# Attention kernel on one Trainium2 core: in four turns of eighteen two key tiles are weighed together, first halves first

## What is computed

```
q, k, v = Wq @ gn(x), Wk @ gn(x), Wv @ gn(x)      # per head: 64 x 2304
attn = softmax(q^T k)                             # 2304 x 2304, no scale
out  = gamma * (attn @ v^T) + Wsc @ gn(x)
y    = x + out
```

## Time and profile before

| | us |
|---|---|
| median of 3 runs | 3061.2 (3058.46 to 3061.65) |
| the profiled execution, its time | 3061.98 |
| the profiled execution, its span | 3060.3 |
| TensorE (PE) busy | 2967.9 (97%) |
| GpSimd (POOL) busy | 2765.5 (90%) |
| VectorE (DVE) busy | 2249.1 (73%) |
| ScalarE (ACT) busy | 1939.8 (63%) |

### The profile page before, as it was taken

The page is one execution under the profiler, slowest core; times in us unless marked ns, Lnnn a source line. Parts: engine busy times, 40 slices in busy tenths (PEclk is TensorE's granted clock), DMA queues, the critical chain, the costliest instruction groups (busy, mean ns, idle before and its releaser), DMA issues. The chain is left out here.

```text
span 3060.3 us, 149786 instructions
## 1 busy us (share of the span) xinstructions
PE 2967.9 (97%) x69035; PEld 2242.4 (73%) x69035; DVE 2249.1 (73%) x2856; ACT 1939.8 (63%) x3156; POOL 2765.5 (90%) x2039
## 2 busy tenths in 40 slices
PE   7999999999999999999999999999999999999998
PEld 4677777777777777777777777777777777777765
DVE  7777677777787767777777767777777777777774
ACT  4565676766566667676656567667666666666555
POOL 1798899999899999999989889999999989999898
PEclk9999999999999999999999999999999999999999
DMA  3111111111112011111011101111010101110101
GB/s 133 32 42 41 31 47 25 47 35 26 35 47 56 24 38 42 34 48 30 21 41 52 48 24 44 38 34 48 21 30 21 30 21 30 22 30 21 30 21 31
DMA packets 169076, 112.71 MB, mean 37 GB/s; under 512 B 120320, under 2 KB 166400, under 8 KB 168448
## 3 DMA queue, kind: packets, MB, share of 16 engines
q1 hardware_dynamic: 168448, 103.13, 12.8%
HBM read 56.10 MB, written 18.87 MB: 24 GB/s over the span
## 5 line engine op out<-in xcount | busy, mean ns | idle before, releaser
L984 POOL TENSOR_TENSOR PLO<-PE 128x768 f16<-128x768 f32 x1727 | 2531.7, 1479 | 226.0 <-ACT PE L613 203.5
L786 DVE TENSOR_REDUCE mx<-MX 128x2 f32<-128x768 f32 x1728 | 1654.6, 958 | 727.0 <-PE MX L444 705.2
L613 ACT ACTIVATE PE<-SL 128x768 f32<-128x768 f32 x1728 | 1400.4, 810 | 1020.2 <-PE SL L470 1020.1
L505 PE MATMUL OB<-V,PE 64*128 64x129 f16 x20736 | 1403.8, 219 | 1.2
L502 PE MATMUL OB<-V,PLO 64*128 64x65 f16 x20736 | 1307.1, 190 | 0.0
L505 PEld LDWEIGHTS OB<-V,PE 64*128 64x128 bf16 x20736 | 1034.4, 94 | 238.4 <-PE OB L502 82.9
L470 PE MATMUL SL<-QK 64*128 64x384 f16 x10368 | 1142.8, 324 | 11.7 <-ACT PE L613 6.5
L502 PEld LDWEIGHTS OB<-V,PLO 64*128 64x128 f16 x20736 | 968.9, 95 | 141.6 <-issue 0.2
L391 PE MATMUL PJ<-X,WT 64*128 64x384 f16 x6624 | 941.0, 323 | 0.0
L444 PE MATMUL MX<-QK 64*128 64x384 f16 x3456 | 579.4, 326 | 46.7 <-DVE mx L786 36.5
L470 PEld LDWEIGHTS SL<-QK 64*128 64x128 f16 x10368 | 440.6, 94 | 180.9 <-ACT PE L613 19.3
(11 more groups left out here) (108 smaller groups left out, 913.8 us busy)
## 6 DMA issues: line engine op xcount, KB each, us to landing
gx<-x SPq DMA_DIRECT2D x36, 768.0 KB, 4.7
xr<-x SPq DMA_DIRECT2D x96, 192.0 KB, 2.4
out<-xr SPq DMA_DIRECT2D x96, 192.0 KB, 1.9
X<-x SPq DMA_DIRECT2D x6, 768.0 KB, 8.5
CR<-c SPq DMA_TRANSPOSE x96, 2.3
back<-half SPq DMA_TRANSPOSE x95, 2.9
QK<-wk SPq DMA_DIRECT2D x1, 1024.0 KB, 12.7
QK<-wv SPq DMA_DIRECT2D x1, 1024.0 KB, 13.4
```

The source lines that it names most:

```text
L505: last = pe.matmul(acc, upper, v, start=begin, stop=False, skip_group_check=True)
L613: act.activation(PE32[:, s % PB, :].rearrange("p (h n) -> p h n", h=2), SL[:, :, 0:CH], ACT.Exp, scale=1.0 / SS).then_inc(s_exp, 1)
L786: nc.vector.tensor_reduce(mx3[:, n % 2, :, k], MX[:, :, 0:CH], AX.X, ALU.max).then_inc(s_mxf, 1)
L984: nc.gpsimd.tensor_tensor(PLO[:, s % PB, :], PE32[:, s % PB, :], PE32[:, s % PB, :].bitcast(BF16)[:, 1:4 * CH:2], ALU.subtract).then_inc(s ...
```

## The change

In a turn k of `STARTS`, TensorE now does score, part 0 of tile s-3, `top`, part 0 of tile s-2, slots. In the turn behind it (1, 5, 10, 14) it does score, part 1 of tile s-4, `top`, slots, part 1 of tile s-3. Both first halves have the same sides, and so have both second halves. `side` and `started` keep the side: a crossing, with its wait, comes only where part 1 has the side of its own part 0. In turn 2, part 1 moves from before the first slot to behind it. `PB` goes from 4 to 5.

```diff
-PB = 4
+PB = 5
...
+            started, side = {}, [0]
...
-                else:
-                    pe.wait_ge(s_half, s + 1)
-                cross = (s + part) % 2
+                    started[s] = side[0]
+                elif side[0] == started[s]:
+                    pe.wait_ge(s_half, len(started))
+                    side[0] = 1 - side[0]
+                cross = side[0]
...
-                    if s >= LAG:
-                        weigh(s - LAG, 0)
-                    if U < TOPS:
-                        top(U)
-                    if s >= LAG and (lo == 0 or k == 2):
-                        weigh(s - LAG, 1)
+                    if lo == 0:
+                        if s >= LAG:
+                            weigh(s - LAG, 0)
+                        if U < TOPS:
+                            top(U)
+                        if s >= LAG:
+                            weigh(s - LAG + 1, 0)
+                    elif k - 1 in STARTS:
+                        if s > LAG:
+                            weigh(s - LAG - 1, 1)
+                        if U < TOPS:
+                            top(U)
+                    else:
+                        if s >= LAG:
+                            weigh(s - LAG, 0)
+                        if U < TOPS:
+                            top(U)
                     for i in range(lo, hi):
+                        if k == 2 and i == lo + 1 and s >= LAG:
+                            weigh(s - LAG, 1)
                         slot(4 * n + b, i)
-                    if s >= LAG and not (lo == 0 or k == 2):
+                    if s > LAG and k != 2 and lo:
                         weigh(s - LAG, 1)
```

## The result

| | before, us | after, us |
|---|---|---|
| median of 4 runs each | 3059.83 (3058.18 to 3061.65) | 3038.91 (3038.01 to 3040.84) |
| span of the profiled execution | 3060.3 | 3039.1 |

The ratio is 0.9932, with a 95% interval of 0.992 to 0.9945: 21 us or 0.7% faster. The forecast was 3046 us, 15 us faster, with a range of 3032 to 3056. The changed kernel ran again with the experiments, ten times: medians 3042.36 (ratio 0.9942, 0.993 to 0.9955) and 3044.05 (0.9947, 0.9933 to 0.9961). Over all 14 runs its median is 3041.5 us, so the gain is 18 to 21 us.

The account below looks back on a forecast made before the run. TensorE's order of work sets the pace, with two turns of every chunk held by another engine. 69 typical chunks x 0.22 = 15 us off 3061.98 gives 3047, median 0.8 lower: 3046 us, range 3032 to 3056.

Parts of the forecast that it names:

- The crossing: TensorE's weight loads wait for OB's own matmuls between part 0 and part 1; covering this saves 0.07 us a turn.
- Turn 9 given back in turn 12: GpSimd's chain holds turn 12's top, so turn 9's 0.07 us comes back as waiting; worth 0.00 to 0.01.
- Turn 2 held in turn 3: OB's evacuation chain ends 0.16 us later against TensorE, turn 3's part 0 waits 0.05; worth about 0.01.
- A typical chunk: Gains 0.07 x 3 (turns 13, 0, 4) + 0.01 (turn 2) + 0.00 (turn 9) = 0.22 us.
- Behind a conversion chunk: In 18 chunks turn 0 waits 0.47 us for GpSimd, absorbed by turn 8's top wait: 0, bounds -0.34 and +0.12.
- The last six chunks: Few slots; score waits for the exponential in 41 places and that loop sets their turns: gain 0.
- Five buffers: Exponential of s waits for part 1 of tile s-5, ended two turns earlier at latest: free; with four not.
- A: Every exposed crossing comes back, 3028 us; a half (turn 9 or 2 kept) gives 3037 to 3041; chance 0.2 together.
- B: More taken back (turn 13's bank wait, 18 chunks, add_result's phase): 3048 to 3053, chance 0.15; no change (3055 to 3060), 0.12.
- C: In turn 11 add_result loses its place between splits and sits out one more: +100 us, 3160; chance 0.05.

Follow-up runs that it names:

- e3: Changed kernel with the pair of tiles given up in turn 9 alone: 3044.09 us, ratio 0.9944.
- e4: Changed kernel with GpSimd's result_lower moved from turn 8 to turn 12 in all chunks: 3045.05 us, ratio 0.9949.
- e11: Changed kernel without add_result's second call, so the lower part of attention's result is left out: 3004.61 us, ratio 0.9822.
- e6: Kernel before the change with GpSimd's result_lower moved from turn 8 to turn 12: 3118.76 us, ratio 1.019.
- e8: Changed kernel with part 1 of turn 2 back in front of the first slot: 3043.94 us, ratio 0.9947.
- e7: Changed kernel with the old order in turn 0 of the 18 chunks behind a conversion chunk: 3041.13 us, ratio 0.9942.
- e1: Kernel before the change with PB = 5 and nothing else: 3059.59 us, ratio 1.0001.
- e2: Changed kernel with PB = 4: 3131.97 us (2 runs), ratio 1.0237.
- e9: Changed kernel with result_lower moved to turn 12, but left in turn 8 of the 18 conversion chunks: 3032.68 us, ratio 0.9911.

## Why the prediction was right, point by point

**The crossing: right, mis-sized.** The term was 0.07 us for turns 0, 4, 9 and 13; they became shorter by 0.082 to 0.087. I had measured only the wait from `top` to part 1 and not the matmuls behind the crossing. The prediction also said that the turns behind the pairs do the same work as before; they are 5 to 12 ns longer, 0.03 us a chunk together.

**Turn 9 given back in turn 12: right.** Said 0.07 back, worth 0.00 to 0.01; measured +0.071 and worth 0.014, shown by e3, e4 and e11. By the rule on the shared port pair (the Trainium skill, SBUF — State Buffer, Who interferes with whom) a VectorE instruction with two SBUF inputs that comes second is blocked until GpSimd's instruction ends. The trace agrees: `add_result` starts beside a split that runs and ends 0.41 us behind it. What I took from the earlier trace rows, that `add_result` always ends behind the first split, does not hold everywhere (e6).

**Turn 2 held in turn 3: right.** Said 0.07 less 0.055; measured 0.078 less 0.059, shown by e8.

**A typical chunk: 0.22 forecast, 0.258 measured.** The crossings gave more than the 0.07 each that the sum had (3 x 0.015 more), and the turns behind the pairs took some of it back.

**Behind a conversion chunk: right.** Said no net gain or loss; the 24 chunks that are or follow one gained 1.6 us together. The wait in turn 0 is 0.49 us where 0.47 was said, 18 times, and `top` of turn 8 waits 0.19 less, where 0.18 was said. e7 shows that giving it up changes nothing.

**The last six chunks: the term was 0, measured 1.1 us.** `score` does wait for the exponential there, but not in every turn.

**The rest.** The two spans differ by 21.2 us. In the two traces the 66 chunks that are not conversion chunks, do not follow one and are not among the last six gained 17.0 us, of which 1.7 are one stretch of lower clock less. The 24 chunks gained 1.6 and the last six 1.1. The first `score` of the main loop comes 1.2 us earlier (86.2 us, where it was 87.4), and 0.4 us lie behind the last one. The earlier start is not the change's: the kernel before with five buffers alone has it too, and the changed kernel's third trace does not (87.6 us). The change's own part is thus 15.3 + 1.6 + 1.1 = 18 us, which is also what the 14 runs give (3060 - 3041.5). The forecast of 15 us had 69 typical chunks of 0.22. So its mechanism holds and its sum is 3 us small; the 21 us of the first comparison have some luck in them.

**Five buffers: right,** free as an addition (e1) and needed (e2). One step of the account is off: part 1 of tile s-5 ends one turn before the exponential of s at the latest, and not two, since tile s-5 can be the first of a pair.

**Rivals.** A (3028 us) fell, since turns 3 and 12 take back what was said. B's terms did not come: turn 13 kept its gain, and turn 8 is at +2 ns. C did not come in this kernel, but it exists: e6 lost 50 us to it, and 12 more to the clock that fell behind it. Its condition was not put rightly: no idle time of GpSimd is needed for `add_result` to get in, as long as the next split has only just become ready.

## What to carry to other kernels

Carry each saved nanosecond forward through the program until another engine's wait holds it: a turn made shorter is worth nothing if a later instruction stands where another engine's queue puts it. An instruction that waits in a strict queue for a busy neighbour can be given cover instead, by putting ready work in front of it; this was worth more here than the change under study. And work that is moved within a queue goes where the queue has room: the same move gave 9 us less where it was left out of the conversion chunks (e9, a part of it the clock's) and none where it was not (e4), and it cost 58 us in the kernel before (e6).

## What the runs showed of the hardware

A VectorE instruction with two inputs in SBUF can sit out not only the GpSimd instruction that runs but up to three more that follow it without a gap: 1.46 us became 4.85 us. It ended 0.41 to 0.45 us behind the end of a GpSimd instruction in every case, and took 0.61 us alone. In the six traces it got in between two splits where the second had been ready for 0.044 us or less (once 0.068), and did not get in at any of the 44 places in e6 at which that was 0.11 us or more. There are counterexamples on the other side: behind a split in turn 11 of the chunk after the statistics it got in with 0.7 to 1.7 us, and behind the shorter conversions (0.91 us) with 0.5 to 0.95 us. What decides between these cases is open; no run here isolates it.
